# Issuing half of a kernel's SBUF-to-SBUF gather DMAs from GpSimd's queue instead of SyncE's

## What is computed

```python
# block 0: adaptive layer norms, cross attention (16 heads of 16), residual
xq, xkv = ada_ln(x, cond), ada_ln(ctx, cond)            # ctx: 8 x 375 x 256
q, k, v = xq @ Wq + bq, *split(xkv @ Wkv + bkv, 2)
x = x + softmax(q k^T / 4) v @ Wp + bp
# block 1: self attention (gated), cross attention over the raw ctx, MLP (gated)
m = silu(cond) @ ada_w + ada_b                          # shifts, scales, gates
x = x + gate_msa * (mha(qkv(ln(x)*(1+scale)+shift)) @ self_o_w + self_o_b)
x = x + mha(q(ln(x)), kv(ctx)) @ cross_o_w + cross_o_b
x = x + gate_mlp * (gelu(h @ mlp_w1 + mlp_b1) @ mlp_w2 + mlp_b2)
```

## Time and profile before

| | us |
|---|---|
| median of 3 runs | 539.46 (538.98 to 542.21) |
| profiled execution, whole time | 543.47 |
| span of its trace, first to last instruction | 541.7 |
| TensorE busy | 457.9 (85%) |
| VectorE busy | 290.5 (54%) |
| ScalarE busy | 250.3 (46%) |
| GpSimd busy | 183.7 (34%) |

### The profile page before, as it was taken

One profiled execution on the slowest core, in us unless ns is written; L12 is line 12 of the kernel. 1 busy time (PEld: TensorE's weight loads), 2 busy tenths in 40 slices (PEclk: granted clock), 3 DMA queues, 4 the chain that ended last, 5 costly groups with the idle time before them and its releaser, 6 DMA issues.

```text
span 541.7 us, 11662 instructions
## 1 busy us (share of the span) xinstructions
PE 457.9 (85%) x4306; PEld 325.8 (60%) x4306; DVE 290.5 (54%) x784; ACT 250.3 (46%) x555; POOL 183.7 (34%) x245
## 2 busy tenths in 40 slices
PE   5765778989899879879797867898988987999996
PEld 5532454657575456556665644566656655678995
DVE  7717447471847544633766738745653543644321
ACT  1442455643555536555442323566665654572221
POOL 3233133463245425525141404244333413243200
PEclk9968698987999979999886868999999989999999
DMA  8667953472334275656817020746174032110000
GB/s 227 163 109 113 220 119 74 104 152 68 52 96 82 57 127 92 89 90 84 111 50 90 10 44 19 191 111 100 33 119 92 17 73 85 30 45 17 19 17 18
DMA packets 48927, 46.13 MB, mean 85 GB/s; under 512 B 12767, under 2 KB 47071, under 8 KB 48871
## 3 DMA queue, kind: packets, MB, share of 16 engines
q1 hardware_dynamic: 45951, 45.12, 42.8%
q10 hardware_dynamic: 2920, 0.27, 0.5%
HBM read 14.57 MB, written 0.93 MB: 29 GB/s over the span
## 4 chain that ended last, share of the span: by engine, by line
PE 60%; DVE 12%; issue 12%; ACT 6%; DMA 4%; POOL 3%; SPq 2%; ACTq 0%; POOLq 0%; DVEq 0%
PE bank L443 8%; PE bank L451 7%; DVE nmax L929 7%; PE bank L582 7%; PE bank L545 6%; PE bank L562 6%; PE bank L477 5%; PE bank L633 5%; PE bank L622 5%; PE bank L607 2%; PE bank L595 2%; ACT xt L683 2%; PE bank L500 2%; ACT prob L774 2%; DMA q_stack_all<-nm_t 2%
## 5 line engine op out<-in xcount | busy, mean ns | idle before, releaser
L929 DVE TENSOR_REDUCE nmax<-bank 112x1 f32<-112x375 f32 (+1 forms) x288 | 141.9, 549 | 101.8 <-PE bank L545 101.1
L774 ACT ACTIVATE prob<-bank 128x448 f32<-128x448 f32 (+2 forms) x224 | 116.4, 544 | 80.0 <-PE bank L562 75.5
L545 PE MATMUL bank<-k_stack,q_stack_all 96*128 96x375 bf16 x256 | 68.1, 350 | 24.0 <-issue 10.8
L1068 POOL TENSOR_TENSOR fill_space<-fill_space 128x375 f32<-128x375 f32 x32 | 29.9, 934 | 117.3 <-ACT fill_space L706 117.3
L562 PE MATMUL bank<-q_stack_all,k_stack 99*128 99x112 bf16 x768 | 55.7, 217 | 7.0 <-DMA q_stack_all<-nm_t 6.9
L451 PE MATMUL bank<-wkv,fill_space 128*128 128x256 f32 (+1 forms) x192 | 53.2, 418 | 9.5 <-ACT xt L683 7.1
L545 PEld LDWEIGHTS bank<-k_stack,q_stack_all 96*128 96x128 bf16 x256 | 24.6, 103 | 58.1 <-DVE nmax L929 21.8
L443 PE MATMUL bank<-fill_space,wkv 128*128 128x375 f32 x128 | 54.6, 555 | 3.1 <-ACT fill_space L706 2.3
L582 PE MATMUL bank<-prob,v_tokens 128*17 128x112 f32 (+1 forms) x1536 | 57.0, 266 | 0.1
L562 PEld LDWEIGHTS bank<-q_stack_all,k_stack 99*128 99x128 bf16 x768 | 41.7, 100 | 24.7 <-issue 13.4
L1082 POOL TENSOR_TENSOR v_tokens<-v_tokens,bias_rows_v 128x256 f32<-128x256 f32 (+1 forms) x48 | 33.5, 713 | 44.4 <-ACT v_tokens L718 44.4
(11 more groups left out here) (120 smaller groups left out, 687.9 us busy)
## 6 DMA issues: line engine op xcount, KB each, us to landing
k_stack<-fill_space SPq DMA_DIRECT2D x192, 93.8 KB, 3.5
q_stack_all<-q_part SPq DMA_DIRECT2D x72, 112.0 KB, 4.2
k_stack_all<-ctx_norm SPq DMA_DIRECT2D x24, 112.0 KB, 5.0
k_stack_all<-in_L_xcond_mlp_w_dram SPq DMA_DIRECT2D x2, 1024.0 KB, 7.8
k_stack_all<-in_L_xcond_ada_w_dram SPq DMA_DIRECT2D x1, 1536.0 KB, 16.8
ctx_tokens<-in_ctx_dram SPq DMA_DIRECT2D x2, 512.0 KB
fill_space<-gate_rows SPq DMA_DIRECT2D x2, 448.0 KB, 3.6
fill_space<-gate_rows SPq DMA_DIRECT2D x1, 896.0 KB, 5.3
```

What stands on the lines that cost most here:

```text
L545: last = pe.matmul(to[:, o:o + w], q_all[0:DEEP, q + h * N2:q + h * N2 + P], keys, start=True, stop=True)
L774: act.activation(prob[n % 4][0:rows, :], bank[SCORE_T[n % 2]][0:rows, 0:GH * T], ACT.Exp).then_inc(exp_done, 1)
L929: dve.tensor_reduce(nmax[:, g * hs:(g + 1) * hs], bank[SCORE[n % 3]][0:T, 0:hs * w].rearrange("t (h k) -> t h k", k=w), AX_X, ALU.max, neg ...
L1068: pool.tensor_tensor(kr[:, m, :], kf[:, m, :], kp[i % 2][:, 0, m, :], ALU.subtract).then_inc(krest_done, 1)
```

## The change

The wait and the six DMAs of `("D", i, c)` become a function of the issuing engine. SyncE calls it for half 0 only; GpSimd calls it for half 1, at the same place of the table, (a, 12). The bytes, the waits and the semaphores are the same.

```diff
@@ pool_step
             pool.tensor_tensor(full[k][:, :, :], full[k][:, :, :], part[k][:, 0, :, :], ALU.subtract).then_inc(rest_done[k], 1)
+        elif kind == "D" and step[2] == 1:
+            stack_k(pool, step[1], 1)
         elif kind == "m" and step[1] >= 2:
...
+    def stack_k(eng, i, c):
+        if i < 2:
+            eng.wait_ge(ones_k, 32)
+            eng.wait_ge(padded, 2)
+        if i >= 2:
+            before = i - 2 if i < B + 2 else i - 2 + B
+            eng.wait_ge(st_psum, UNITS_TO[before] + (NG * NT // 2) * (c + 1))
+        load_k(eng, i, c)
+
     def sp_step(sp, step):
         kind = step[0]
-        if kind == "D":
-            _, i, c = step
-            if i < 2:
-                sp.wait_ge(ones_k, 32)
-                sp.wait_ge(padded, 2)
-            if i >= 2:
-                before = i - 2 if i < B + 2 else i - 2 + B
-                sp.wait_ge(st_psum, UNITS_TO[before] + (NG * NT // 2) * (c + 1))
-            load_k(sp, i, c)
+        if kind == "D" and step[2] == 0:
+            stack_k(sp, step[1], 0)
```

## The result

| | before | after |
|---|---|---|
| median of the runs | 539.22 us | 547.42 us |
| ratio, 95% interval | | 1.0155 [1.01, 1.021] |
| span of the profiled execution | 541.7 us | 545.3 us |
| mean granted TensorE clock | 0.911 | 0.911 |
| GpSimd busy | 183.7 us | 233.0 us |

The kernel is about 1.5% slower, 8.2 us by the medians. (A ratio is formed over the undisturbed runs, so it need not be the quotient of the medians.) The predicted value, 546.5, is 0.9 us off. Its working is mostly not what happened.

A forecast was written before the change was run, and what follows sets the result against it. The prediction took TensorE, working through its table in order, to bound the kernel. Late second halves 5.0, bias after attention 7 0.2 and two queues 1.8 made 7.0 us, so 539.5 + 7.0 = 546.5 us, range 538 to 562.

The forecast's parts named there:

- GpSimd's issue at 1.04 us: Each K stack DMA issue on GpSimd costs 1.04 us, like its dearest ordinary instruction; six take 6.2 us instead of 3.7.
- the issue is cheap: Rival, chance 0.30: at 0.6 to 1.0 us per GpSimd issue the kernel stays within 1%.
- Landing 2.3 us behind the issue: A second half's last DMA lands 2.3 us after GpSimd's issuing ends, 8.5 us after it begins.
- Late second halves, 5.0 us: At head 8, seven items' second halves come 0.2 to 2.1 us late; less item 6's gain, 5.0 us.
- Item 6, 1.5 us gained: Item 6's second half lands at 189.1 instead of 190.60, so TensorE gets it 1.5 us earlier.
- Nothing queued behind on GpSimd: In item 11, GpSimd's work behind the six issues starts later but costs nothing, up to 1.37 us per issue.
- The 0.2 us after attention 7: After attention 7, GpSimd's issues and bias end at 261.9, and VectorE's L964, due at 261.71, loses 0.2 us.
- VectorE's casts: Rival, chance 0.04: cast L917 holds up GpSimd's issuing in five items by up to 0.91 us, 4.5 us more, 551.
- Two queues at once, 1.8 us: In items 2, 14 and 15 GpSimd's issuing meets SyncE's first half: 0.6 us each, 1.8 us.
- The front: Rival: in items 0 and 1 SyncE's queue is free some 7 us earlier, worth 0 to 2 us either way.
- The range and the chances: Range 538 to 562 us; slower by over 1% 0.60, within 1% 0.36, faster 0.04.
- the prediction's own signs of being wrong: Issue under 1.0 or over 1.3 us, landing much over 2.3, or first halves over 0.6 us later in many items.

The follow-up runs named there:

- e6: The kernel before, all DMAs on SyncE, with GpSimd doing the wait and four small unread powers where its six issues would stand: 537.62 us, ratio 1.003.
- e0: The kernel before, unchanged, profiled once more on a second chip: 540.65 us.
- e7: Against the kernel before, GpSimd issues second halves of items 10 to 15 only, waiting until four of six first-half DMAs have landed: 537.93 us, ratio 1.0004.
- e8: Against the kernel before, GpSimd issues the second halves of items 10 to 15 only, without holding back: 548.79 us, ratio 1.0143.
- e3: Against the changed kernel, GpSimd issues the second halves of items 0 and 1 only, SyncE the others: 539.86 us, ratio 1.0049.
- e1: The changed kernel itself again, unchanged, on another chip: 550.86 us, ratio 1.0235.
- e2: Against the changed kernel, GpSimd waits in every item until four of the first half's six DMAs have landed: 547.16 us, ratio 1.0156.

## Why the number was right and its working wrong

*What bounds the kernel*: right. It is TensorE working through its table, and the loss came where TensorE stands at a head whose half has not landed. That the first halves are later than the second, and that the profile's "issue" is a transfer, was also read rightly, and it was the place to look.

*GpSimd's issue at 1.04 us*: wrong, 0.512. A compute instruction of that engine says nothing of a DMA issue on it. The premise of the rival "the issue is cheap" held, and the lower bound of the range of prices, 0.59, was not low enough. By the prediction's own sum this price would have meant no change: no half late, 2.3 us back in item 6, 1.8 lost to two queues.

*Landing 2.3 us behind the issue*: too short. Where nothing overlapped (items 3, 4, 5, 7, 10, 12) it was 3.1 to 3.4 us. A half has landed 6.2 to 6.5 us after GpSimd begins, not 8.5. The 2.3 were read from the smallest of item 3's six landings, 2.9 us, though the same row has the last one at 3.6.

*Late second halves, 5.0 us*: wrong in every one of its seven terms, by these two dates. In items 3, 5, 7, 10, 11, 12 and 15 TensorE's matmuls don't wait at head 8. In items 3 and 10 the half lands 0.1 to 0.2 us ahead of them, so it had no time to spare.

*Item 6, 1.5 us gained*: wrong. Its DMAs and head 8 (against the earlier trace rows):

```profile
L1161 POOL DMA_DIRECT2D k_stack<-fill_space x6: 512/512/530, 183.2 to 185.9; - x6
...
DMA to landing us min/median/max: 3.1/3.5/7.1
...
193.02 0.33 PE L545 MATMUL bank<-k_stack,q_stack_all 96*128 96x375 bf16 x1 [2.07 <-DMA k_stack<-fill_space]
```

The issuing took 3.2 us instead of 7.1, a gain larger than foreseen, but the slowest DMA landed 7.1 us after its start, and the wait is 2.07 us instead of 2.32. Beside GpSimd's six, SyncE now issued the loads for the next layer (SP timeline of after):

```profile
183.56 2.34 SPq L1214 DMA_DIRECT2D bias_rows<-in_L_xcond_self_o_b_dram  x1
```

Before, the bias loads stood behind the K half on SyncE and were first issued 7.1 us after its first DMA. Now they begin 0.35 us after it, into the same DMA engines. That they are what delays the half is read from these dates; no run moved them alone. The prediction had costed what stands behind the removed issues at nothing, by asking only when it is needed. It should have asked what it collides with.

*Nothing queued behind on GpSimd*: right up to attention 7, and e6 shows it for 2.7 us in all items. The 0.2 us after attention 7 did not come either, since the issues took 3.03 us there.

*VectorE's casts*: the earlier trace rows has the cast L917 at 0.91 us beside a GpSimd instruction. Item 10's cast falls in the issuing that begins at 354.53 (DVE timeline of after):

```profile
354.62 0.39 DVE L917 CAST q_part<-q_full 128x448 bf16<-128x448 f32 x1 [1.15 <-POOL q_full L1086]
```

It takes 0.39 us, as it does alone. The issue beside it took 0.588 us, and in items 3, 5, 7 and 12, with the same cast beside the first issue, 0.589 to 0.595; first issues without it took 0.512 to 0.706. So neither held the other up noticeably. The Trainium skill's rule on the shared port ("SBUF — State Buffer", section "SBUF: two separate sides") is not borne out by this trace for these DMAs and this cast of 0.39 us; a longer one no run shows.

*Two queues at once, 1.8 us*: the step that failed by its size, and the one that carries nearly the whole result. It was priced as one foreign transfer, 0.6 us, in each of items 2, 14 and 15. The runs show 7.6 us between items 10 and 15 alone. Three things were missing. First, the delay is a share and not a queue place: GpSimd's six transfers run beside all of SyncE's that are not yet landed, so item 15's last landing behind the issue went from 2.4 (2.8 in e0) to 5.1 us, 2.3 to 2.7 more and not 0.6. Second, the dates were taken with the slow issue; more important, only the start of GpSimd's issuing was compared with SyncE's last issue, not with its last landing 3 us later. By landing dates the first half is still moving in items 11, 12 and 13 too, though only item 13's landed later for it, by 0.6 us. Third, the prediction had no term for the clock: 0.7 of the 5.7 us between before and after in this stage, and 4.7 of the 11.5 between e7 and e8.

The rule that bore on this is in the Trainium skill, "DMA: Bandwidth & Descriptors", section "Issuing engines are not separate DMA queues": the queues of all engines share the same 16 DMA engines, so a second one saves time to issue and brings no bandwidth. The traces agree (item 0's twelve DMAs landed by 40.3 us with two queues and by 40.6 with one), and they add what it can cost. The single queue had in effect been an order too: with it item 0's first half, which is needed first, landed 6.7 us after its first issue, with two queues 11.4.

*The front*: the rival spoke of 0 to 2 us either way. It lost 1.9 to 2.5 us at item 0's head 0 and 4.4 to 5.0 by item 2, by the late first half and the later return of the clock. In e3 all of this was back by item 4; in after 2 us were not, and in e1 6.

*The range and the chances*: slower by over 1% had 0.60, and that is what came. But the mechanism given for it, late second halves, was false, and the case that was true had been priced at a quarter. The value came out right by luck: 5.2 us that did not come and 6.4 us that were missing nearly cancel. All three of the prediction's own signs of being wrong were there: the issue took under 1.0 us, the landing 0.8 to 1.1 us more than 2.3, and seven of the first halves (items 0, 1, 2, 9, 13, 14, 15) landed over 0.6 us later.

Open: the share that each queue gets of the engines, what decides how long the clock stays low, and why item 4 to 8 varies from 175 to 181 us between executions of kernels that don't differ there.

## What to carry to other kernels

Before moving a DMA to an idle queue, compare first uses: if the moved transfer is needed later than one that can still be in flight, it takes engine time from the one that TensorE stands for. Count a transfer as in flight until its last landing, not until its issue. Where two queues are wanted, hold the later-needed one back by a wait on the earlier one's landing, at a place where the waiting engine has nothing else due (so in e7, not in e2). Price a new wait of TensorE at its length and allow for more, since the clock can be low for longer with it: it added 0.7 us to 5.0 in the change and 4.7 to 6.8 in e8.

## What the runs showed of the hardware

- GpSimd issues a DMA of 93.8 KB from 64 partitions to 16 in 0.512 us, back to back in 3.0 to 3.1 us for six. SyncE takes 0.595 and 3.7. Undisturbed, the last lands 3.1 to 3.4 us behind the end of the issue on GpSimd's queue and mostly 2.3 to 3.5 on SyncE's.
- GpSimd's queue moved its 9.22 MB in 4608 packets, 48 for each DMA, and the program's DMA packets fell from 48927 to 45855.
- Twelve transfers on two queues finish no earlier than twelve on one (40.3 and 40.6 us in item 0). Beside GpSimd's six, the first half lands 11.4 us after its first issue instead of 6.7.
- A clock of 0.50 that lasted to 38.6 us in the kernel before lasted to 45.4 with a wait of 2.26 us at head 0 in it, and eight matmuls behind the wait took 2.99 us instead of 1.51. Behind item 15's head 0 a wait of 2.71 us was followed by 3.7 us at 0.54 in one execution of the kernel before, and one of 2.10 us by 11.0 us at 0.53 in the other.
